# Four chunks of score maxima move from the unit work ahead of a batch into the batch's first attention head

## The reference

```
xn  = adaln(x, c, g1, w_ada1, b_ada1)                 # rmsnorm, scale and shift from the condition
qkv = bitlinear(xn, w_qkv, b_qkv).reshape(B, T, 3, H, hd)
q, k, v = (qkv[:, :, i].transpose(0, 2, 1, 3) for i in range(3))
attn = softmax(einsum('bhqd,bhkd->bhqk', q, k) * hd ** -0.5)
o = einsum('bhqk,bhkd->bhqd', attn, v)
x = x + bitlinear(o, w_proj, b_proj)
xn = adaln(x, c, g2, w_ada2, b_ada2)
x = x + bitlinear(gelu(bitlinear(xn, w_fc1, b_fc1)), w_fc2, b_fc2)
```

## Time and profile before

| | us |
|---|---|
| median of three runs | 2755.3 |
| lowest and highest run | 2752.84 and 2759.84 |
| the profiled execution | 2761.85 |
| its span in the trace | 2760.0 |
| TensorE busy in it | 2642.9 |
| VectorE busy in it | 2145.9 |
| GpSimd busy in it | 1963.7 |
| ScalarE busy in it | 1841.7 |

### The profile page before, as it was taken

How to read it: one execution, slowest core, us unless ns; L and a number is a source line. 1 busy time by engine, 2 the same in 40 slices (tenths; PEclk the granted TensorE clock), 3 DMA queues, 4 the chain that set the end, 5 groups by cost and what they waited for, 6 DMA issues and landing times. The chain is left out here.

```text
span 2760.0 us, 60668 instructions
## 1 busy us (share of the span) xinstructions
PE 2642.9 (96%) x22062; PEld 1504.1 (54%) x22107; DVE 2145.9 (78%) x4435; ACT 1841.7 (67%) x3323; POOL 1963.7 (71%) x1579
## 2 busy tenths in 40 slices
PE   9999999999999999999879999999999999998998
PEld 8655566555765547655445554555455445544443
DVE  4877778776787767877667778777877787768997
ACT  3466665666556665666556677667766776667996
POOL 0298854897459863698749986987789788965542
PEclk8999999999999999999989999999999999999999
DMA  7122353224432335223232313321432132245444
GB/s 237 40 59 60 114 170 109 59 59 150 135 100 60 79 124 166 76 60 105 77 81 64 77 33 112 81 57 31 120 82 59 44 108 59 59 166 182 104 104 111
DMA packets 170353, 260.48 MB, mean 94 GB/s; under 512 B 85437, under 2 KB 93253, under 8 KB 169161
## 3 DMA queue, kind: packets, MB, share of 16 engines
q1 hardware_dynamic: 168264, 250.27, 33.3%
q0 software_dynamic: 1792, 6.33, 0.6%
HBM read 99.15 MB, written 38.88 MB: 50 GB/s over the span
## 5 line engine op out<-in xcount | busy, mean ns | idle before, releaser
L555 DVE TENSOR_REDUCE a_mxs<-ps 128x1 f32<-128x512 f32 x2048 | 1269.1, 682 | 248.2 <-PE ps L420 245.7
L514 ACT ACTIVATE a_p<-ps 128x512 f32<-128x512 f32 x2048 | 1043.7, 606 | 197.5 <-PE ps L434 188.3
L374 POOL TENSOR_TENSOR a_sum<-a_p 128x512 f32<-128x512 f32 x736 | 939.2, 1286 | 197.7 <-PE ps L454 111.3
L420 PE MATMUL ps<-a_k,a_q 96*128 96x512 f32 x2048 | 852.9, 422 | 16.1 <-DVE a_mxs L555 14.6
L434 PE MATMUL ps<-a_q,a_k 98*128 98x512 f32 x2048 | 808.4, 419 | 15.2 <-ACT a_p L514 7.6
L454 PE MATMUL ps<-a_sum,a_unit 128*32 128x512 f32 x1536 | 652.2, 598 | 0.6 <-POOL a_sum L374 0.6
L380 POOL TENSOR_TENSOR a_sum<-a_sum,a_p 128x512 f32<-128x512 f32 x480 | 618.6, 1289 | 37.7
L454 PE MATMUL ps<-a_p,xv 128*32 128x512 f32 x3968 | 640.5, 597 | 0.0
L420 PEld LDWEIGHTS ps<-a_k,a_q 96*128 96x128 f32 x2048 | 387.2, 189 | 253.0 <-DVE a_mxs L555 101.7
L434 PEld LDWEIGHTS ps<-a_q,a_k 98*128 98x128 f32 x2048 | 384.4, 189 | 240.7 <-ACT a_p L514 143.5
L523 ACT ACTIVATE a_ots<-ps 128x512 f32<-128x512 f32 x256 | 152.6, 598 | 405.5 <-PE ps L454 404.5
(11 more groups left out here) (256 smaller groups left out, 3158.8 us busy)
## 6 DMA issues: line engine op xcount, KB each, us to landing
a_q<-qh SPq DMA_DIRECT2D x256, 128.0 KB, 2.3
a_k<-kh SPq DMA_DIRECT2D x256, 128.0 KB, 2.4
a_q<-ql SPq DMA_DIRECT2D x128, 128.0 KB, 2.4
a_k<-kl SPq DMA_DIRECT2D x128, 128.0 KB, 2.4
x<-a_p SPq DMA_DIRECT2D x64, 256.0 KB, 2.2
a_p<-in_w_fc SPq DMA_DIRECT2D x12, 1024.0 KB, 7.8
kh<-in_x SPq DMA_DIRECT2D x4, 2048.0 KB, 14.6
a_p<-x SPq DMA_DIRECT2D x16, 512.0 KB, 6.0
```

The costliest lines, as they stand in the source:

```text
L374: pair = pool.tensor_tensor(tile, keys[0], keys[1], ALU.add)
L420: pe.matmul(self.mx[self.mx_ring[at]], self.q[j][0:96, t * P:(t + 1) * P], self.k[j][0:96, half * HALF:(half + 1) * HALF], start=True, sto ...
L514: act.activation(self.key_tile(u, kt), self.st[self.st_ring[CHUNKS * k + n]], ACT.Exp, scale=self.scale).then_inc(self.s_exp, 1)
L555: dve.reduce_max(self.mxs[:, k % 2, c:c + 1], self.mx[self.mx_ring[CHUNKS * k + c]], axis=AX.X).then_inc(self.s_mxr, 1)
```

## The change

An `Attention` that is made with `apart=True`, the second layer's, gets a `PRELUDE` of 12 in place of 14: 24 chunks are done in the unit work. A new method `chunks_at(k, s)` says which chunks stand in step s of head k. In steps 0 to 3 of head 0 it gives three chunks (8 to 15 of head 1, 0 to 3 of head 2), in all other steps the two that stood there. TensorE's step puts the third chunk behind the second pair of score and chunk; VectorE's step reduces three. `m_parts` for head 1 keeps its place behind step 2.

In the unit work of batches 1 to 3 the parts keep their products and QK14 and QK15 have none. In that of batch 0 the parts follow the last 12 products in place of the last 14, so each part stands two products later. `MT` and `MROW` stay 9 and 11.

```diff
@@ class Attention, __init__
+        if apart:
+            self.PRELUDE = CHUNKS - 4
@@
+    def chunks_at(self, k, s):
+
+        if self.PRELUDE < CHUNKS - 2 and k == 0 and s < STEPS // 2:
+            first = 2 * self.PRELUDE + 3 * s
+            some = range(first, first + 3)
+        else:
+            first = CHUNKS * k + 2 * (CHUNKS - 2) + 2 * s
+            some = range(first, first + 2)
+        return [(n // CHUNKS, n % CHUNKS) for n in some]
@@ run_pe
-                a = 1 if s < 2 else 2
                 after_values = s in (3, 7)
-                for r in range(2):
-                    if ok(k) and not after_values:
+                some = self.chunks_at(k, s)
+                for r in range(len(some)):
+                    if ok(k) and r < 2 and not after_values:
                         self.scores(pe, N, k, s, r, NQ * b + i + k // NJ)
-                    if ok(k + a):
-                        self.max_chunk(pe, N + a, k + a, (2 * s + r + CHUNKS - 4) % CHUNKS, NQ * b + i + (k + a) // NJ)
-                    if ok(k) and after_values:
+                    of, c = some[r]
+                    if ok(of):
+                        self.max_chunk(pe, N + of - k, of, c, NQ * b + i + of // NJ)
+                    if ok(k) and r < 2 and after_values:
                         self.scores(pe, N, k, s, r, NQ * b + i + k // NJ)
@@ run_dve
-                a = 1 if s < 2 else 2
...
-                for c in range(2):
-                    if ok(k + a):
-                        self.reduce_chunk(dve, N + a, k + a, (2 * s + c + CHUNKS - 4) % CHUNKS)
+                for c, (of, chunk) in enumerate(self.chunks_at(k, s)):
+                    if ok(of):
+                        self.reduce_chunk(dve, N + of - k, of, chunk)
@@ layer1a, products, batches 1 to 3
-                chunks = QK[9:11] + V[LEAD:] + QK[11:12] + T_ + QK[12:]
+                chunks = QK[9:11] + V[LEAD:] + QK[11:12] + T_ + QK[12:14]
```

## The result

| | before | changed |
|---|---|---|
| median of nine runs (us) | 2754.09 | 2762.97 |
| lowest and highest | 2752.69 and 2759.84 | 2759.14 and 2768.47 |
| the profiled execution | 2761.85 | 2762.06 |
| its span | 2760.0 | 2760.3 |
| mean granted clock in it | 0.985 | 0.988 |

The ratio is 1.0034, with a 95% interval of 1.0025 to 1.0042: by the medians the changed kernel is 8.9 us slower, and the interval is 6.9 to 11.6 us. The forecast was 2763.8 us, the range 2757 to 2770.

What follows compares the result with a forecast made beforehand. The prediction took head 0 to be bound by VectorE's reductions up to the values rounds, by TensorE from there on. 3 x 0.90 + 4.6 + 1.2 = 8.5 us on the median 2755.3 gave 2763.8 us, range 2757 to 2770.

Steps and rivals of the forecast that it cites:

- The place and the sign: Second layer, unit work and first head of batches 0 to 3: slower, 2.7 us in three batches, 4.6 and 1.2 in batch 0.
- The late row: Ahead of batch 0: m_row falls behind ScalarE's pair for QK15, so the first score comes 2.83 us later.
- Rival (a): Batch 0: something hides the late row, only four reductions are paid; 5.1 us in all, 2760.4 us, chance 0.18.
- The reductions of batch 0: Head 0 of batch 0: four more reductions ahead of the values rounds; with the late row, values 4.6 us later.
- The clock: Head 0 of batch 0: after 5.6 us idle TensorE's granted clock falls to 0.5, adding 1.2 us (0 to 2.5).
- Batches 1 to 3: First head of each: four reductions cost 2.40 us, VectorE starts 1.50 earlier; +0.90 us a batch, +2.7 in three.
- the squares: Ahead of batches 1 to 3: ScalarE's eight squares, 0.66 us apart, let VectorE's first reduction start only 1.50 us earlier.
- the lower bound of 0.55: Batches 1 to 3: cost of 0.55 us a batch, were the squares no slower behind the additions than before.
- Rival (b): The clock also falls in the other three stretches' first heads, longer in batch 0: 13.5 us, 2768.8 us, chance 0.17.
- Rival (c): Chunks don't hold head 0; the earlier 1.5 us a batch is gained whole, batch 0 costs 2.8: 2753.6 us, chance 0.08.
- Rival (d): Over 0.3% faster: late row hidden, unit work of batch 0 1.3 us shorter, later heads lose waits; 2746.5 us, chance 0.05.

Runs made afterwards that it cites:

- Experiment 3: The changed kernel with batch 0's maxima transposed behind part 8 and their row written behind part 9: 2757.75 us, ratio 1.0014 to the kernel before.
- the others alone: The kernel before with the change in batches 1 to 3 only, batch 0 keeping its 28 chunks ahead: 2758.81 us, ratio 1.0020.
- the filler kernel: The changed kernel with 20 more filler matmuls in TensorE's idle time ahead of batch 0's first score: 2765.38 us, ratio 1.0043 to the kernel before.
- batch 0 alone: The kernel before with the change in batch 0 only, batches 1 to 3 keeping their 28 chunks ahead: 2760.11 us, ratio 1.0027.
- the row early: The same run as Experiment 3: the changed kernel with batch 0's row of maxima written behind part 9, 2757.75 us, ratio 1.0014 to the kernel before.
- the other four: The others alone (1.0020), and with VectorE's wait for the squares moved to step 7 of head 0: kernel before (0.9998), changed (1.0025), the others alone (1.0004).
- the changed kernel with the squares later: The changed kernel with VectorE's wait for ScalarE's squares moved behind step 7 of head 0 in batches 1 to 3: 2762.26 us, ratio 1.0025.
- experiment 4: The same run as the filler kernel: 20 more filler matmuls ahead of batch 0's first score in the changed kernel, 2765.38 us, ratio 1.0043.

## Why the prediction was right

**The place and the sign: right.** The three stretches and batch 0 carry the loss, and nothing shows in heads behind the first. The sum was 8.5 us; the traces show 7.4, the runs 8.9 (6.9 to 11.6).

**The late row: right, its size within 0.2 us.** Forecast: m_row 2.34 us ahead of the first score, which comes 2.83 us later against the old order. Shown: 2.38 and 2.70. The gain ahead of it was a little larger than worked out: QK14 is dequantized 22.59 us behind V0 where it was 24.05, 1.46 us earlier in place of 1.30. Experiment 3 undid this step alone, and the first score moved by 4.01 us. Rival (a), that something hides the row, falls with it.

**The reductions of batch 0: right.** Forecast from V0 to the values: 28.50 + 9.06 + 4.6 + 1.2 = 43.4 us. Shown: 43.07.

**The clock: right, 1.09 us in place of 1.2.** The granted clock fell to 0.50 in the course of 5.44 idle us, and filling them brought 1.09 us back. With them filled the head takes 10.78 us, and the forecast without the clock's term was 1456.32 - 1445.51 = 10.81. The Trainium skill, "TensorE: Matmul & The Clock Gate", Part 1 ("What's actually happening"), has the clock halve behind idle time and return under sustained work. The trace agrees, 0.50 in one window and 0.99 in the next. About 4.5 us at half the clock cost only 1.09 us here, since VectorE sets the pace of that head.

**Batches 1 to 3: the mechanism right, one term mis-sized.** The prediction gave + 2.40 for the four reductions, and 2.40 is shown. It gave - 1.50 for the earlier start, and 1.84 is shown. The failed term is the squares. Their pitch of 0.66 us was read in the earlier trace rows from squares that waited for VectorE's additions: each starts 0.03 us behind the end of its addition there, so the squares went at the additions' pace (0.66 us, and 0.86 for the last three). It was used for a stretch in which they would wait for nothing. There they go (1703.81 - 1699.52) / 7 = 0.61 us apart, and the last one starts 1.81 us earlier against QK12, not 1.50. The additions end as forecast (6.50 us long in place of 5.97, since they now go at the pace of Y's products), so the wait for the squares did not grow to near 1.2 us, it stayed at 0.81. The net is +0.6 us a batch in place of +0.9 (0.60, 0.51 and 0.75), near the lower bound of 0.55. That bound assumed the squares no slower behind the additions than before, which is what happened: what was given as a bound was the case.

**Rival (b)**, falls of the clock in the three other heads, did not show in the changed kernel's trace, and showed once, for 1 us, in experiment 3. More low clock elsewhere is another matter, below. **Rival (c)**, nothing lost, needed idle time among head 0's reductions; there is none. **Rival (d)** asked for shorter heads behind the first: there are none.

**What the sum leaves open.** The traces ask for 7.4 us, the runs for 8.9. The runs' own mean granted clocks point at the rest. The nine runs of the changed kernel have 0.9863 on average (0.985 to 0.989), the 54 runs of the kernel before that were timed beside the experiments 0.9885 (0.986 to 0.991). Among the runs of one kernel, a mean clock lower by 0.001 went with about 1.7 us more (a straight line through all 136 runs whose clock is on record, each taken against its kernel's mean). So 0.0022 stands for some 3.7 us, an estimate. The fall at batch 0's first score (0.66, 0.50 and 0.99 in three windows of 4 us) is 0.0012 of it and cost 1.09 us; the other 0.0010 is some 1.7 us, about what is missing. By the same estimate the others alone (0.9870 against 0.9887) have 2.9 us beside the 1.9 of their heads, 4.8 in all where the ratio says 5.5, and the filler kernel (0.9862) has 4.3 beside 6.0, 10.3 where the ratio says 11.8. The average of nine runs is uncertain by about 0.0004, so this is likely and not shown.

Where the low clock lies, single traces can only hint at. The part behind the last score, which the change does not touch, takes 299.5 us before and 302.3 in the changed kernel; it takes 302.3 too with batch 0 alone and with the filler, 299.8 with the row early, and 299.0 to 299.1 in the other four. It goes with the granted clock in 2460 to 2480 and 2480 to 2500: 0.91 and 0.83 before, 0.77 and 0.80 in the changed kernel, 0.90 and 0.68 with batch 0 alone, 0.86 and 0.72 with the filler, 0.91 and 0.91 in those four. The late first score does not decide it alone, since the changed kernel with the squares later has it as well. By what route the change makes such falls likelier, if it does, is not settled here.

## What to carry to other kernels

When work moves from in front of a loop into its first round, look first for indices that are tied to positions: here two numbers that stayed the same put a row of maxima behind the last pair of ScalarE, and that cost more than the moved work (undoing it took 4.4 us off V0 to values, of 5.5). Work that a bound engine does later is paid in full (four reductions, 2.40 us a batch), less what the engine ahead of it really comes earlier, and that gain should be read from rows in which nobody waits. A pitch read from instructions that wait for their producer is too long for a stretch in which the producer is done.

## What the runs showed of the hardware

- Runs of one kernel spread by more than the change is worth: the kernel before took 2749.83 to 2762.31 us in 28 runs. This goes with their mean granted clock (0.986 to 0.991), and in the profiled executions with falls of TensorE's clock in places that no edit touches; by V0 of the second layer two executions with the same work up to there were 9.86 us apart.
- The same wait can be followed by a fall or by none: TensorE waited 1.90 us up to 704.65 in the kernel before and 1.90 up to 704.36 in the changed one, 2.17 us up to 1042.83 and 2.17 up to 1037.59. Behind both waits the clock fell in the kernel before (0.79 in 704 to 712 and in 1040 to 1048) and stayed at 1.00 in the changed one.
- A fall does not need a long wait: with the row early, TensorE waited 1.30 us for the DMA and then 0.41 us, and the clock was 0.69 in the next window; in the kernel before, a wait of 1.27 us at the same place was followed by no fall. Windows of the kernel before, behind its first score at 1442.68 (us, TensorE busy, clock, DMAs):

```profile
1444.00:1448.00 4.00, 3.22 (x13) 1.00 0.51 114
1448.00:1452.00 4.00, 3.76 (x17) 1.00 0.01 2
```

- A fall costs little where another engine sets the pace: 1.09 us for about 4.5 us at half the clock in the head that VectorE binds.
- Taking away one fall did not shorten the run (experiment 4): another one stood later in its trace.
